# First layer's recurrence: clamp behind the exponential, six reciprocals through ACT's inverse root and a Newton step, matmuls ahead of the first sum

## The reference

```python
tf = sigmoid(sum(time_emb))                       # one number for each batch
decay = exp(-exp(w)) * (0.5 + 0.5 * tf)
ek = exp(minimum(k, 30.0)); ekv = ek * v
# a and b: forward scans of ekv and ek with decay; the same backward
num = nf + nb - ekv + exp(minimum(u + k, 30.0)) * v
den = df + db - ek  + exp(minimum(u + k, 30.0))
out = sigmoid(x) * (num / maximum(den, 1e-8)) * (0.8 + 0.2 * tf)
```

## Time and profile before

| | |
|---|---|
| median of 3 runs | 472.46 us (472.36 to 475.43) |
| profiled execution | 472.23 us |
| its span, first to last instruction | 470.5 us |
| mean granted TensorE clock | 0.985 of full |
| busy: PE, DVE, POOL, ACT | 401.1, 341.2, 239.7, 235.0 us |

### The profile page before, as it was taken

One profiled execution on the slowest core, in us unless ns is written; L12 is line 12 of the kernel. 1 busy time (PEld: TensorE's weight loads), 2 busy tenths in 40 slices (PEclk: granted clock), 3 DMA queues, 4 the chain that ended last, 5 costly groups with the idle time before them and its releaser, 6 DMA issues.

```text
span 470.5 us, 5885 instructions
## 1 busy us (share of the span) xinstructions
PE 401.1 (85%) x1678; PEld 254.6 (54%) x1685; DVE 341.2 (73%) x619; ACT 235.0 (50%) x471; POOL 239.7 (51%) x336
## 2 busy tenths in 40 slices
PE   2577899999999999956784889999999999986795
PEld 1465578655455555624562346566566555663453
DVE  5999887999999999789958347547745510128995
ACT  4600276166667766657976122332332332329884
POOL 6544042578778997324000646775775474114642
PEclk9999999999999999989997799999999999999999
DMA  7900001655565643000021798899899987050001
GB/s 227 399 4 0 1 2 36 222 175 176 185 218 186 212 168 135 0 1 2 1 89 44 245 417 323 288 335 338 306 309 365 308 282 274 25 190 0 13 33 47
DMA packets 23264, 77.39 MB, mean 164 GB/s; under 512 B 3424, under 2 KB 7904, under 8 KB 19648
## 3 DMA queue, kind: packets, MB, share of 16 engines
q1 hardware_dynamic: 19936, 69.94, 42.2%
q0 software_dynamic: 2208, 6.03, 3.9%
q10 hardware_dynamic: 1088, 1.05, 0.7%
HBM read 71.76 MB, written 5.24 MB: 164 GB/s over the span
## 4 chain that ended last, share of the span: by engine, by line
PE 33%; issue 5%; DVE 4%; DMA 4%; ACT 4%; POOL 1%; SPq 0%; POOLq 0%; ACTq 0%; DVEq 0%
PE bank L1874 16%; PE bank L1894 10%; PE bank L1885 2%; DVE gl L1485 2%; DMA gu<-in_gu 1%; DVE pt L1492 1%; PE bank L1860 1%; ACT q2T L801 1%; PE bank L1753 1%; PE bank L1734 1%; PE bank L1928 1%; DMA xb<-cond_rows,row_i 1%; DMA gy<-y_rows 1%; PE bank L1745 1%; DMA cond_rows<-cond 1%
## 5 line engine op out<-in xcount | busy, mean ns | idle before, releaser
L1874 PE MATMUL bank<-gu,xbT 128*128 128x512 f32 x184 | 83.2, 595 | 3.4 <-issue 1.8
L1664 PE MATMUL bank<-hx,w2raw 128*128 128x512 f32 x128 | 67.3, 607 | 4.1 <-DVE hx L1220 3.2
L1421 DVE TENSOR_TENSOR hm<-bank,sl 128x512 f32<-128x512 f32 x23 | 15.9, 691 | 69.8 <-issue 33.0
L746 ACT ACTIVATE rl<-bank 128x512 f32<-128x512 f32 x64 | 38.1, 595 | 40.1 <-PE bank L1528 39.1
L1874 PEld LDWEIGHTS bank<-gu,xbT 128*128 128x128 f32 x184 | 34.5, 190 | 38.3 <-issue 35.1
L532 POOL DMA_INDIRECT xb<-cond_rows,row_i x23 | 26.1, 1133 | 53.5 <-DVE row_i L1371 37.4
L1526 PE MATMUL bank<-xlhi,w1hi 128*128 128x512 f32 x64 | 49.4, 771 | 0.0
L1894 PE MATMUL bank<-dn,hT 128*128 128x256 f32 x184 | 45.2, 388 | 3.4 <-ACT hT L877 0.7
L457 POOL TENSOR_TENSOR fw<-fw,bw 128x256 f32<-128x256 f32 x32 | 24.2, 757 | 42.7 <-DVE bw L1024 42.2
L1220 DVE TENSOR_TENSOR hx<-bank,cwb 128x512 f32<-128x512 f32 x64 | 41.9, 658 | 4.3 <-ACT bank L750 4.1
L539 POOL DMA_INDIRECT y_rows<-yb,dest_i x23 | 25.1, 1090 | 35.6 <-ACT yb L883 34.5
(11 more groups left out here) (294 smaller groups left out, 904.4 us busy)
## 6 DMA issues: line engine op xcount, KB each, us to landing
gu<-in_gu SPq DMA_DIRECT2D x23, 1024.0 KB
cwb<-cw_rows SPq DMA_DIRECT2D x32, 512.0 KB, 3.9
dn<-in_dn SPq DMA_DIRECT2D x23, 512.0 KB, 4.7
traw<-in_t SPq DMA_DIRECT2D x3, 1024.0 KB
w1raw<-in_w SPq DMA_DIRECT2D x8, 256.0 KB, 4.9
w2raw<-in_w SPq DMA_DIRECT2D x8, 256.0 KB, 4.5
kT<-in_kt SPq DMA_DIRECT2D x4, 256.0 KB, 5.2
x<-in_x SPq DMA_DIRECT2D x2, 512.0 KB, 6.8
```

Of the source, the lines that this page charges most:

```text
L746: act.activation(rl[:, u % 3, :], bank[u % 4][:], ACT.Relu).then_inc(sem("r_ready"), 1)
L1664: pe.matmul(bank[4 + s][:], w2raw[:, e // 4 % 2, e % 4, :], hx[:, 0, u % 4, :], start=(e == 0), stop=(e == E0 - 1), skip_group_check=True) ...
L1874: ins = pe.matmul(bank[2 * (b % 2) + up][:], xbT[:, b % 2, k, :], gu[:, b % RING, k, up * I2:up * I2 + I2], start=(k == 0), stop=(k == KC ...
```

## The change

- ACT takes the exponentials straight from k as the DMA delivers it, with u as bias for `exp(u + k)`. DVE clamps the results at exp(30) (`clip_key`, `clip_bonus`), two units at a time: batch 0 around unit 0's scans, batches 1, 2 and 3 (`clips`) at the ends of units 0, 1 and 2. POOL takes over the product ek x k of batch 0 as well.
- The reciprocals of units 2 to 7 are made in two parts. ACT computes 1/sqrt of the denominator's sum and squares it (`first_inverse`). DVE makes one Newton step in two instructions (`newton_product` after part 1 of the next unit, `newton_step` after part 2) and the gain in a third (`newton_gain` after part 3). Its sign is turned by a negative factor in `make_cond`. Units 0 and 1 keep DVE's reciprocal.
- The denominator's sum alternates between two PSUM banks.
- The decay columns for the first layer are computed straight into PSUM. The full `dec` and `ubk` tables follow after part 1 of unit 0 (`side_columns`).
- POOL's two early `wkv_kup` move behind `side_value(3)` and `route_consts`, ahead of `first_value(2)`. Their exponentials on ACT move behind the table load for the experts.
- ACT issues the three small DMAs (te, wl, ul), which SP issued between the first and the second load of k.
- ACT loads the inverse root's table after the sigmoid of x, and `sm_hi` comes after the inverse of unit 2. The table for the sigmoid is loaded again after unit 7.
- PE runs 18 matmuls of the identity with itself (128 columns, float32) before unit 0's first sum.
- Some semaphores of the second and the fourth layer are merged (`q1T3_ready` into `q1T_ready` and the like), with counts moved by 8 tiles.

```diff
+DIVIDED = 2
...
-        def first_sum(d):
-
-            return bank[(4, 7)[d]][:, 0:S]
+        def first_num_sum():
+
+            return bank[4][:, 0:S]
+
+        def first_den_sum(n):
+
+            return bank[(7, 5)[n % 2]][:, 0:S]
...
-                if b == 0:
-                    for dst, src in ((te, te_d), (wl, w_d), (ul, u_d)):
-                        sp.dma_start(dst[:], src).then_inc(sem("small_in"), 16)
...
+                pool.wait_ge(sem("euk_ready"), n // 2 + 1)
                 wait(pool, sem("sum_num"), n - 1)
                 pool.tensor_tensor(eu[:, n % 2, 0, :], first_euk(n), kT[:, n, :], ALU.mult).then_inc(sem("euv_ready"), 1)
...
-            pool.wait_ge(sem("kup_ready"), 1)
-            wkv_kup(NBLK, 1, 0)
-            wkv_kup(NBLK + 1, 2, 0)
+            side_value(0)
             first_value(0)
             first_value(1)
             for b in range(1, B):
                 side_value(b)
             route_consts()
+            pool.wait_ge(sem("te_sum"), 2)
+            wkv_kup(NBLK, 1, 0)
+            wkv_kup(NBLK + 1, 2, 0)
             for n in range(2, NBLK):
...
+            for dst, src in ((te, te_d), (wl, w_d), (ul, u_d)):
+                act.dma_start(dst[:], src).then_inc(sem("small_in"), 16)
             act.wait_ge(sem("small_in"), 48)
...
             def side_exp(b):
-                act.wait_ge(sem("kmin_ready"), b + 1)
-                act.activation(ekk[:, 2 * b:2 * b + 2, 1, :], ekk[:, 2 * b:2 * b + 2, 1, :], ACT.Exp).then_inc(sem("ek_ready"), 1)
+                act.wait_ge(sem(f"kT_in{b}"), 16)
+                act.activation(ekk[:, 2 * b:2 * b + 2, 1, :], kT[:, 2 * b:2 * b + 2, :], ACT.Exp).then_inc(sem("ek_raw"), 1)
...
             def first_exp(n):
-                act.wait_ge(sem("kup_ready"), n + 1)
-                act.activation(first_euk(n), first_euk(n), ACT.Exp).then_inc(sem("eu_ready"), 1)
+                act.activation(first_euk(n), kT[:, n, :], ACT.Exp, bias=ul[:, 0, n % KC:n % KC + 1]).then_inc(sem("eu_raw"), 1)
+
+            def first_inverse(n):
+
+                act.wait_ge(sem("sum_den"), n + 1)
+                act.activation(fw[:, n % 2, 1, :], first_den_sum(n), ACT.Abs_reciprocal_sqrt, bias=tiny[:],
+                               scale=2.0 ** -14).then_inc(sem("r0_ready"), 1)
+                act.wait_ge(sem("r0_ready"), 2 * (n - DIVIDED) + 1)
+                act.activation(fw[:, n % 2, 1, :], fw[:, n % 2, 1, :], ACT.Square, scale=2.0 ** -7).then_inc(sem("r0_ready"), 1)
 
             for b in range(B):
                 side_exp(b)
                 first_exp(2 * b)
                 first_exp(2 * b + 1)
-            wkv_exp(NBLK, 0)
-            wkv_exp(NBLK + 1, 1)
             sigmoid_x(0)
-            act.wait_ge(sem("sm_in"), 16)
-            act.activation(sm_hi[:], sm_raw[:], ACT.Copy).then_inc(sem("sm_high"), 1)
+            act.wait_ge(sem("consts"), 5)
+            act.activation(table[:, 7:8], tiny[:], ACT.Abs_reciprocal_sqrt)
+            for n in range(DIVIDED, NBLK):
+                if n == 6:
+                    cond_high(0, (0,))
+                first_inverse(n)
+                if n == DIVIDED:
+                    act.wait_ge(sem("sm_in"), 16)
+                    act.activation(sm_hi[:], sm_raw[:], ACT.Copy).then_inc(sem("sm_high"), 1)
+            load_table(0, ACT.Sigmoid)
...
             load_table(4, ACT.Exp)
+            wkv_exp(NBLK, 0)
+            wkv_exp(NBLK + 1, 1)
             expert_relu(0)
...
-            def side_exp(b):
-
-                dve.wait_ge(sem(f"kT_in{b}"), 16)
-                dve.tensor_scalar(ekk[:, 2 * b:2 * b + 2, 1, :], kT[:, 2 * b:2 * b + 2, :], 30.0, None, ALU.min
-                                  ).then_inc(sem("kmin_ready"), 1)
-
-            side_exp(0)
+            def clip_key(b):
+
+                dve.wait_ge(sem("ek_raw"), b + 1)
+                dve.tensor_scalar(ekk[:, 2 * b:2 * b + 2, 1, :], ekk[:, 2 * b:2 * b + 2, 1, :], E30, None, ALU.min
+                                  ).then_inc(sem("ek_ready"), 1)
+
+            def clip_bonus(b):
+
+                dve.wait_ge(sem("eu_raw"), 2 * b + 2)
+                dve.tensor_scalar(GT[:, 1, 2 * b:2 * b + 2, :], GT[:, 1, 2 * b:2 * b + 2, :], E30, None, ALU.min
+                                  ).then_inc(sem("euk_ready"), 1)
+
+            def clips(b):
+                clip_key(b)
+                clip_bonus(b)
...
+            chain(dve.tensor_tensor(bank[6][:, 0:NBLK].rearrange("p (b k) -> p b k", k=KC),
+                                    wl[:, 0:1, :].to_broadcast([P, B, KC]),
+                                    per_b[:, 2, 0, :, :].to_broadcast([P, B, KC]), ALU.mult))
+
+            def side_columns():
+
+                dve.tensor_tensor(dec[:], wl[:].rearrange("p l (o k) -> p l o k", o=1).to_broadcast(lbk),
+                                  per_b[:, 2, :, :, :].to_broadcast(lbk), ALU.mult)
+                dve.tensor_copy(ubk[:], ul[:].rearrange("p l (o k) -> p l o k", o=1).to_broadcast(lbk)).then_inc(sem("te_sum"), 1)
+                dve.tensor_scalar(tfb[:, 3, :], tfb[:, 0, :], 0.2, 0.8, ALU.mult, ALU.add)
+                chain(dve.tensor_scalar(tfb[:, 1, :], tfb[:, 0, :], -0.2, -0.8, ALU.mult, ALU.add))
...
+            def newton_product(n):
+
+                dve.wait_ge(sem("r0_ready"), 2 * (n - DIVIDED) + 2)
+                dve.wait_ge(sem("euv_ready"), n + 1)
+                dve.scalar_tensor_tensor(out=first_euk(n), in0=fw[:, n % 2, 1, :], scalar=1e8, in1=first_den_sum(n),
+                                         op0=ALU.min, op1=ALU.mult).then_inc(sem("newton"), 1)
+
+            def newton_step(n):
+
+                dve.wait_ge(sem("newton"), 2 * (n - DIVIDED) + 1)
+                dve.scalar_tensor_tensor(out=first_euk(n), in0=first_euk(n), scalar=2.0, in1=fw[:, n % 2, 1, :],
+                                         op0=ALU.subtract, op1=ALU.mult).then_inc(sem("newton"), 1)
+
+            def newton_gain(n):
+
+                dve.wait_ge(sem("sum_num"), n + 1)
+                dve.wait_ge(sem("newton"), 2 * (n - DIVIDED) + 2)
+                dve.scalar_tensor_tensor(out=GT[:, 0, n, :], in0=first_euk(n), scalar=-1e8, in1=first_num_sum(),
+                                         op0=ALU.max, op1=ALU.mult).then_inc(sem("G_ready"), 1)
+
+            def quotient(n, part):
+
+                if n < 0:
+                    return
+                if n < DIVIDED:
+                    step = {2: first_reciprocal, 3: first_gain}.get(part)
+                else:
+                    step = {1: newton_product, 2: newton_step, 3: newton_gain}.get(part)
+                if step:
+                    step(n)
+
+            between = {(0, 1): [lambda: clip_bonus(0), side_columns], (0, 3): [lambda: clips(1)],
+                       (1, 3): [lambda: clips(2)], (2, 3): [lambda: clips(3)],
                        (5, 3): [lambda: make_cond(0, 0), lambda: make_cond(0, 1)],
                        (6, 2): [lambda: cond_low(0, 0, 0)], (6, 3): [lambda: cond_low(0, 0, 1)]}
             dve.wait_ge(sem("consts"), 4)
-            first_kup(0)
-            first_kup(1)
-            for part in range(2):
-                wkv_scan(0, 0, 0, 0, part)
-            side_next(1)
-            side_value_0()
+            clip_key(0)
             for n in range(NBLK):
                 for part in range(4):
-                    if n or part >= 2:
-                        wkv_scan(n, 0, n, n % 2, part)
-                    if n and part == 2:
-                        first_reciprocal(n - 1)
-                    if n and part == 3:
-                        first_gain(n - 1)
+                    wkv_scan(n, 0, n, n % 2, part)
+                    quotient(n - 1, part)
                     for step in between.get((n, part), ()):
                         step()
+            newton_product(NBLK - 1)
+            newton_step(NBLK - 1)
             make_cond(0, 2)
-            first_reciprocal(NBLK - 1)
-            first_gain(NBLK - 1)
+            newton_gain(NBLK - 1)
...
+                total = first_den_sum(n) if d else first_num_sum()
+                if d == 0:
+                    wait(pe, sem("G_ready"), n)
+                elif n - 2 < DIVIDED:
+                    wait(pe, sem("rden_ready"), n - 1)
+                else:
+                    pe.wait_ge(sem("newton"), 2 * (n - 2 - DIVIDED) + 1)
+                pe.matmul(total, ident[:], fw[:, n % 2, d, :], start=True, stop=False)
+                pe.matmul(total, ident[:], bw[:, n % 2, d, :], start=False, stop=False)
+                if d == 0:
+                    pe.wait_ge(sem("euv_ready"), n + 1)
+                else:
+                    pe.wait_ge(sem("euk_ready"), n // 2 + 1)
+                pe.matmul(total, ident[:], last, start=False, stop=True).then_inc(sem("sum_" + part), 1)
...
+            keep_going(bank[3][:, 0:P], 18, ident[:], ident[:])
             for n in range(6):
```

More of the change, by code:

```diff
@@ L12 @@
+import math
 from contextlib import ExitStack
@@ L49 @@
 ROUTED_SCALE = 2.5
```

(45 more changed lines are left out.)

56 lines of the change are left out of this document (19 added, 37 removed).

## The result

The changed kernel took 478.49 us (median of 6 runs, 477.62 to 481.39), the kernel before 474.51 beside it (6 runs). The ratio is 1.0097 with an interval of 1.0067 to 1.0127, so 3.2 to 6.0 us were lost. The prediction had +0.9 us and a range that ended at 478.0. It added the 0.9 to 472.46; on the 474.51 that stood beside the changed kernel it would have come to 475.4. The profiled execution measured 479.43 us, with a span of 477.7 and a mean granted clock of 0.957 (before 0.985).

What follows compares the result with a forecast made beforehand. DVE's list was taken to bound the first 51 us, PE after it. The terms 0.3 - 4.7 + 0.9 + 2.7 + 1.4 gave +0.6, taken as +0.9, so 473.3 us; range 468 to 478.

Steps and rivals of the forecast that it cites:

- the small loads' term: Start of the first layer: loads issued from ACT bring the first scan 0.7 us earlier; bounds 0.3 lost, 1.0 gained.
- +0.6: End of the first layer's recurrence: the summed terms make it 0.6 us later than before.
- The wait behind POOL: Ahead of unit 2's Newton product: DVE idles 5.0 us for POOL's value; with the start's gain, +0.3 net.
- - 4.7 + 0.9 + 2.7 + 1.4: Recurrence terms in us: six shorter units, small waits and unit 7's exposed inverse, the step behind the split, the clock.
- The step behind the split: Unit 2's Newton step, both operands in SBUF, waits for POOL's whole weight split: 2.7 us lost.
- The clamps' 1.48 us: Slow clamp length before the change, said to agree with the SBUF exclusion rule; the forecast priced clamps at 0.42.
- The units: Units 2 to 7: a reciprocal (1.65) replaced by product and step (2 x 0.43), -0.79 each, six times -4.7 us.
- The clock: PE's clock falls during the wait for POOL, slowing the sums before unit 3's product: +1.4 us.
- nearly +3 if the step is not held by the split: Alternative size of the low clock's cost before unit 3's product, in place of +1.4 us.
- That the wait doesn't bind: Faster rival: POOL's value for unit 2 comes early, -8.0 us, so 464.5; chance 0.08.
- both rivals: Two tables loaded per unit on ACT, 9.6 us more, 483, chance 0.03; clamps at 1.48 us, +3.2, 476.5, chance 0.10.
- the slow return: Slower rival: PE's clock stays low through unit 6, 4.8 us more, 478; chance 0.10.

Runs made afterwards that it cites:

- e1: The changed kernel with the three small loads issued by SP again, between the first and second load of k: 475.33 us, ratio 1.0025.
- e5: The kernel before with only the load move: ACT issues the three small loads, SP the four loads of k in a row: 476.26 us, one run.
- e11: The changed kernel, with SP holding the second load of k and everything after it until the small loads have landed: 475.58 us, one run.
- e2: The changed kernel with POOL's constants and two early additions moved behind the split of the first expert weights: 472.76 us, ratio 0.9979.
- e9: e4 with POOL making unit 2's value ahead of the product for batch 3: 465.43 us, ratio 0.9812.
- e4: e3 with the Newton product left in the PSUM bank of the denominator's sum, and the wait for POOL's value moved to the step: 466.83 us, ratio 0.9832.
- e6: The changed kernel without the 18 matmuls ahead of the first sum: 474.23 us, one run.
- e8: The changed kernel with 20 more identity matmuls on PE between unit 2's denominator and numerator: 478.53 us, one run.
- e3: The changed kernel with the edits of e1 and e2 together: 468.96 us, ratio 0.9901.
- e7: e3 with all eight reciprocals on DVE: no inverse root, Newton step or third table load: 469.06 us, ratio 0.9892.

## Why the prediction was wrong

**The step that failed is the small loads' term**: "0.7" gained, with a loss of 0.3 as the worst bound. Measured, the wait for ul went from 4.71 to 7.11, 2.4 us later, and the first scan from 7.21 to 9.16, 1.95 later. DMA issues of the changed kernel (line, engine, KB each, median us to landing, first 12 us):

```profile
kT<-in_kt SPq DMA_DIRECT2D x4, 256.0 KB, 4.6
x<-in_x SPq DMA_DIRECT2D x2, 512.0 KB, 6.6
...
te<-in_te ACTq DMA_DIRECT2D x1, 128.0 KB, 3.9
...
wl<-in_w ACTq DMA_DIRECT2D x1, 4.0 KB, 4.2
ul<-in_u ACTq DMA_DIRECT2D x1, 4.0 KB, 5.4
```

ul took 2.5 us on SP in the kernel before. There it stood behind one of k's loads of 256 KB and ahead of the other three and of x. On ACT it is issued at 1.72 us, and SP issues all four of k's loads by 2.6 us and then x meanwhile. I had counted the issue time that the move saves. The bound of 0.3 for the sharing was a guess with no row behind it. The same view of the kernel before had k at 5.2 us to landing and x at 6.8, the nearest rows for a load that shares the engines. e1, e5 and e11 show it from three sides. The Trainium skill, page "DMA: Bandwidth & Descriptors", section "Issuing engines are not separate DMA queues", says that DMAs from ACT, SP and POOL run on the same 16 engines and interleave. The runs agree (ul at 7.11 with SP's loads beside it, at 5.05 with them held); it was the rule that spoke against this part of the change, and I had not weighed it.

From here the sum can be closed at the marker, where the forecast was +0.6 (its +0.9 is for the time, with 0.3 behind the marker). Three differences lead to the measured +3.2:
- The first scan comes 1.95 later in place of 0.7 earlier: 2.65 more. From the first scan to unit 3's it is 14.21 us, from 18.32, so 4.1 less where I had 3.5: 0.6 back. The wait behind POOL is 0.2 longer. Together 2.3.
- From unit 2's product to the marker it is 25.73 us, where the prediction's terms give 25.4 (the 25.1 from unit 2's reciprocal to the last gain before, - 4.7 + 0.9 + 2.7 + 1.4): 0.3 more.
- 0.6 + 2.3 + 0.3 = +3.2.

The loads' chain carries nearly all of the miss. In time the changed kernel is 5.2 us above the forecast of 473.3. Of these, 2.05 are the kernel before itself, whose median beside it is 474.51 and not 472.46, 2.6 are the miss at the marker, and the rest is the open one at the end of this section. So that the time ended just outside the range, and not inside, is partly chance.

The other steps:
- **The wait behind POOL** was right in place, releaser and length: 5.0 predicted, 5.22 measured, 0.74 in e2 and gone in e9. Its end hangs on DVE's own clamp of batch 3, so it hides no delay of the start: the late loads move it with everything else (e1).
- **The step behind the split** was right: 2.7 predicted, 2.5 more than 0.40 measured. In e9 the step reads one operand from PSUM and takes 0.40 beside the same split. The rule of the Trainium skill's page "SBUF — State Buffer" that the prediction weighed is borne out by that pair (2.90 in the changed kernel, 0.40 in e9). The clamps' 1.48 us, which I had called in agreement with it, are no case of it: a clamp has one tensor input, and at 8.39 it took 0.40 while POOL ran `wkv_kup` (7.14 to 9.98). What I missed is a second held step, at 45.10: 1.45 us, so 1.05 more, beside `w1lo`.
- **The units**: from unit 3's product to unit 4's it is 3.43 us, 0.95 less than 4.38, where I had 0.79. The product and the step hold DVE for 0.31 and 0.32 us each, from their start to the next instruction's, where I had taken 0.43. Over six units this would be 1.0 us more gain than I took, which pays for the second held step.
- **The clock** fell as said (0.85 from 24 to 26 us, then 0.50 until 34) and cost nothing where I put it, on top of the held step. ACT's inverse of unit 3 ended at 35.40, before DVE came to the product at 35.82. I had counted the whole numerator's sum behind the wait, but its forward and backward parts don't need POOL's value. The note "nearly +3 if the step is not held by the split" was right: e4 has 2.65. PE's timeline of the changed kernel has only the `eu` part behind it:

```profile
29.81 1.22 PE L1664 MATMUL bank<-eu,ident 128*128 128x256 f32 x2 [5.77 <-POOL eu L454]
...
31.68 1.06 PE L1658 MATMUL bank<-fw,ident 128*128 128x256 f32 x2
...
48.20 0.67 PE L1658 MATMUL bank<-fw,ident 128*128 128x256 f32 x2 [2.31 <-DVE GT L1124]
...
50.69 1.06 PE L1658 MATMUL bank<-fw,ident 128*128 128x256 f32 x2
```

- **A second fall**, which I had not foreseen, took its place. After 2.31 us of idle PE is back at 48.20, and from 49.6 its pairs take 1.06 again (granted clock 0.82 from 48 to 50 us, 0.50 from 50 to 52). The product of unit 7 then waits 2.17 us for ACT, and unit 6's gain to unit 7's is 4.02 us against 2.34 in e1: 1.7 us. e1 and e6 have the same 2.31 and 2.32 us of idle there and no fall, e8 and e11 have one (2.31 and 2.32). And in e3 the clock is at 0.56 from 22 to 24 us, with an idle of 1.28 us there. What decides it stays open. So the clock's 1.4 came out near its size for another reason.
- **From unit 2's product to the last gain** the 25.73 against 25.4 is partly luck: the clock's 1.4 was not paid and the units gave 1.0 more, while the second fall took 1.7 and the second held step 1.05.
- **The rivals.** That the wait doesn't bind was priced at -8.0 us. With the wait, the held step and the loads mended, e9 is 10.1 us ahead of the kernel before at the marker and 6.8 to 11.0 us in time (its interval on 474.94). So the price was right to within some 2 us, and the condition wasn't met. ACT loads no table between inverse root and square in any unit, and the clamps took 0.40 to 0.43, most of them started just ahead of POOL's products: both rivals fall. (The page that the prediction cited from the Trainium skill, "ScalarE: Activation LUTs", doesn't name the square among its cheap functions; for the square this trace shows it.) The clock came back by 36 us in the changed kernel, so the slow return falls as well.

Open is a rest. The ratio says 3.2 to 6.0 us, the marker 3.2, and in most variants the time is 1 to 3 us worse against the kernel before than the marker says (e1: +1.2 and -0.5; e2: -1.0 and -3.6; e3: -4.7 and -6.4), but not in e4 (-8.0 and -7.1) or e7. In the profiled pair the spans differ by 7.2 us, 4.0 more than the marker. The last expert block, whose first to last down product take 136.9 us before and 139.5 after, has 2.6 of the difference, and what follows it has 2.0. PE of the changed kernel in that block:

```profile
278.00:280.00 2.00, 0.22 (x2) 1.00 1.00 414
...
282.00:284.00 2.00, 2.00 (x4) 0.50 0.97 397
```

Before, the stretch from 282 us has nine matmuls at 1.00 where this has four at 0.50 (the same time, not quite the same work). Over the runs the loop varies from 136.9 to 140.5 without order by the variant (e3 136.9, e4 140.5). No run isolated it, and whether the changed first layer has a part in it isn't shown.

## What to carry to other kernels

Before a load is moved to another queue, list the large transfers that will be in flight beside it: the place behind or ahead of them may be worth more than the issue time. Where a change lets an engine wait on another's list, the order of that list is part of the change; moving three items there (e2) was worth more than the new arithmetic (e7). Two delays that overlap hide each other: mending one (e4) shows only 0.7 us at the marker until the other is mended as well (e9, 3.0 more).

## What the runs showed of the hardware

- A load of 4 KB took 2.5 us to landing when SP issued it behind one load of 256 KB and ahead of its other large loads (kernel before). From ACT it took 5.4 us with all of them beside it (changed kernel), and 3.3 us with all but the first held (e11).
- A `scalar_tensor_tensor` of 256 elements with both inputs in SBUF took 2.90 us beside a POOL split of 3.02 us (changed kernel). With one input in PSUM it took 0.40 beside a split of 3.03 (e9).
- The same idle of 2.31 to 2.32 us on PE was followed by a fall of the clock in three of five kernels (the changed kernel, e8 and e11; not e1 and e6).
- 4.63 us of fill on PE and then 3.17 us of idle did not keep the clock up (e8: 0.91 from 28 to 30 us, then 0.50).
- The profile prints 1.00 for the granted clock before the first rise, while a pair takes 1.19 us where it takes 0.70 after it (e6 against the changed kernel).
